# Root, scaling and one weight piece moved, context subtractions split between two engines, exponentials kept in PSUM

## The reference

```python
kh = concat([ctx @ wk + bk, bias_k])            # per head, K = 128
vh = concat([ctx @ wv + bv, bias_v])
weights = softmax((h @ wq + bq) @ kh^T / sqrt(K))
x = x + (weights @ vh) @ wo + bo                # h = layernorm(x), layers 1 and 2
x = x + gelu(layernorm(x) @ w_fc1 + b_fc1) @ w_fc2 + b_fc2
```

## Time and profile before

| what | value |
|---|---|
| median of three runs | 1814.93 us (1812.28 to 1815.42) |
| profiled execution | 1819.03 us |
| its span | 1817.2 us |
| VectorE busy | 1180.4 us |
| ScalarE busy | 743.2 us |
| GpSimd busy | 823.0 us |
| PE weight loads (beside matmuls) | 1724.6 us |

### The profile page before, as it was taken

One profiled execution on the slowest core, in us unless ns is written; L12 is line 12 of the kernel. 1 busy time (PEld: TensorE's weight loads), 2 busy tenths in 40 slices (PEclk: granted clock), 3 DMA queues, 4 the chain that ended last, 5 costly groups with the idle time before them and its releaser, 6 DMA issues.

```text
span 1817.2 us, 30212 instructions
## 1 busy us (share of the span) xinstructions
PE 1773.7 (98%) x11146; PEld 1724.6 (95%) x11146; DVE 1180.4 (65%) x2711; ACT 743.2 (41%) x1624; POOL 823.0 (45%) x653
## 2 busy tenths in 40 slices
PE   8999999999999999999999999999999999999999
PEld 4899999999899999998989999998999999999999
DVE  2667666666776665666775666667766656576665
ACT  3644333334443333335443343335433333344554
POOL 2684352353283352532672523532833525325554
PEclk9999999999999999999999999999999999999999
DMA  9833231123441221223521211234412212204342
GB/s 249 241 118 90 66 86 45 49 65 107 112 125 39 55 59 46 77 63 100 144 72 44 74 44 54 60 107 116 120 38 55 60 45 78 63 18 141 117 128 82
DMA packets 116164, 156.89 MB, mean 86 GB/s; under 512 B 48344, under 2 KB 63960, under 8 KB 116020
## 3 DMA queue, kind: packets, MB, share of 16 engines
q1 hardware_dynamic: 113300, 150.68, 29.7%
q10 hardware_dynamic: 2720, 4.30, 0.7%
HBM read 149.81 MB, written 5.14 MB: 85 GB/s over the span
## 4 chain that ended last, share of the span: by engine, by line
PE 79%; DVE 7%; DMA 5%; POOL 4%; ACT 3%; issue 1%; SPq 1%; ACTq 0%; DVEq 0%; POOLq 0%
PE psum L680 25%; PE psum L681 25%; PE psum L682 25%; PE psum L1004 3%; POOL wbuf_lo L597 2%; DMA stage<-head_w_dram 1%; DMA ctxT_in<-ctxT_dram 1%; DMA p_scratch<-p_row 1%; DVE prob L1811 1%; POOL wbuf_hi L553 1%; DVE a_lo L1510 1%; DMA ctx_rows_in<-ctx_dram 1%; ACT prob L1358 1%; POOL kw L581 1%; DVE stats L1802 1%
## 5 line engine op out<-in xcount | busy, mean ns | idle before, releaser
L553 POOL TENSOR_TENSOR wbuf_hi<-stage,zero_col 128x512 fp32r<-128x512 f32 x256 | 270.3, 1056 | 727.5 <-PE psum L682 613.5
L597 POOL TENSOR_TENSOR wbuf_lo<-stage,wbuf_hi 128x512 fp32r<-128x512 f32 x256 | 344.3, 1345 | 20.1
L680 PE MATMUL psum<-pT_hi,ctx_rows_hi 121*128 121x250 f32 (+3 forms) x1152 | 333.9, 290 | 0.0
L681 PE MATMUL psum<-pT_lo,ctx_rows_hi 121*128 121x250 f32 (+3 forms) x1152 | 331.4, 288 | 0.0
L682 PE MATMUL psum<-pT_hi,ctx_rows_lo 121*128 121x250 f32 (+3 forms) x1152 | 331.3, 288 | 0.0
L680 PE MATMUL psum<-ctxT_hi,a_hi 128*125 128x362 f32 (+1 forms) x832 | 281.2, 338 | 0.4
L682 PE MATMUL psum<-ctxT_hi,a_lo 128*125 128x362 f32 (+1 forms) x832 | 274.2, 330 | 0.0
L681 PE MATMUL psum<-ctxT_lo,a_hi 128*125 128x362 f32 (+1 forms) x832 | 274.1, 329 | 0.0
L680 PE MATMUL psum<-a_hi,wbuf_hi 128*128 128x400 f32 x720 | 258.0, 358 | 6.1 <-POOL wbuf_lo L597 4.5
L1510 DVE TENSOR_TENSOR a_lo<-psum,a_hi 128x500 fp32r<-128x500 f32 (+2 forms) x288 | 144.1, 521 | 174.8 <-ACT a_hi L1132 174.7
L681 PE MATMUL psum<-a_lo,wbuf_hi 128*128 128x400 f32 x720 | 250.0, 347 | 0.0
(11 more groups left out here) (196 smaller groups left out, 3465.0 us busy)
## 6 DMA issues: line engine op xcount, KB each, us to landing
stage<-head_w_dram SPq DMA_DIRECT2D x256, 256.0 KB, 2.7
mlp_stage<-mlp_w_dram SPq DMA_DIRECT2D x32, 512.0 KB, 3.5
ctx_rows_in<-ctx_dram SPq DMA_DIRECT2D x20, 726.0 KB
ctxT_in<-ctxT_dram SPq DMA_DIRECT2D x20, 724.0 KB, 6.9
p_b<-p_scratch SPq DMA_DIRECT2D x64, 200.0 KB, 3.6
key_stage<-head_w_dram SPq DMA_DIRECT2D x22, 256.0 KB, 8.8
l0w<-l_w_dram ACTq DMA_DIRECT2D x16, 256.0 KB, 8.6
x_held<-x_scratch SPq DMA_DIRECT2D x4, 800.0 KB, 5.7
```

The costliest lines, as they stand in the source:

```text
L553: return nc.gpsimd.tensor_tensor(out, in_, zero_col[0:in_.shape[0], :].broadcast_to(tuple(in_.shape)), ALU.add)
L597: nc.gpsimd.tensor_tensor(lo, held, hi.bitcast(F32), ALU.subtract).then_inc(stage_free, 1)
L680: pe.matmul(out, a_h, x_hi, start=start, stop=False)
L681: pe.matmul(out, a_h, x_lo, start=False, stop=False)
```

## The change

The pieces: q4 comes in step (0, 0) instead of (0, 1). GpSimd's context rows of batches 1 to 3 each come one weight later. The context subtractions are cut into parts: the rows into 3 of 512, the columns into 4 of 362. In three of the four phases GpSimd takes over the columns of batches 0 and 1 of the phase that follows, near the end of the phase; VectorE keeps those of batch 2 (behind k0) and 3 (now in step (0, 2)). The semaphore of the columns' low parts becomes one for each batch.

The exponentials are written back into the bank of the scores, and VectorE scales from there into `prob`. The wait for the transposes of two blocks ago goes from the exp to the scaling, and the scores' wait for their bank goes from the exp to the scaling.

In the step (5, 2) ScalarE does hidden_roots ahead of the second exp; in (5, 3) ctx_rows_hi of batch 0 goes to the end of the step and ctx_columns_hi of batch 1 comes there from behind the last attended_hi. On VectorE, at both steps, a part of attended_lo comes ahead of each invert or scale, and the fourth of these behind probs_lo.

```diff
-    (0, 0, "a"): "q3", (0, 1, "a"): "k3", (0, 1, "b"): "q4", (0, 2, "a"): "k4",
+    (0, 0, "a"): "q3", (0, 0, "b"): "q4", (0, 1, "a"): "k3", (0, 2, "a"): "k4",
...
-ROWS_LO_BEHIND = {9: 1, 10: 2, 11: 3}
+ROWS_LO_BEHIND = {10: 1, 11: 2, 12: 3}
...
             def ctx_rows_lo(use, b):
-                at = slice(3 * b, 3 * b + 3)
                 pool.wait_ge(cr_hi_s, use * NB + b + 1)
-                nc.gpsimd.tensor_tensor(r_lo[0:CH, at, :], r_in[0:CH, at, :], r_hi[0:CH, at, :].bitcast(F32),
-                                        ALU.subtract).then_inc(cr_lo_s, 1)
+                for at in range(3 * b, 3 * b + 3):
+                    done = nc.gpsimd.tensor_tensor(r_lo[0:CH, at, :], r_in[0:CH, at, :], r_hi[0:CH, at, :].bitcast(F32),
+                                                   ALU.subtract)
+                done.then_inc(cr_lo_s, 1)
+
+            def ctx_columns_lo(use, b):
+                pool.wait_ge(ct_hi_s, use * NB + b + 1)
+                ctx_b = slice(b * T, (b + 1) * T)
+                for c in range(DC):
+                    done = nc.gpsimd.tensor_tensor(c_lo[:, c, ctx_b], c_in[:, c, ctx_b], c_hi[:, c, ctx_b].bitcast(F32),
+                                                   ALU.subtract)
+                done.then_inc(ct_lo_s[b], 1)
...
                         if ph + 1 < len(PHASES):
+                            ctx_columns_lo(ph + TURNS, 0)
                             ctx_rows_lo(ph + TURNS, 0)
+                    if i == W_AT["v", H - 2] and ph + 1 < len(PHASES):
+                        ctx_columns_lo(ph + TURNS, 1)
...
-                    wait(pe, s_exp, ph * S_LAYER + i - 1)
+                    wait(pe, s_norm, ph * S_LAYER + i - 1)
...
                     act.wait_ge(s_max, ph * S_LAYER + i + 1)
-                    if i >= 2:
-                        act.wait_ge(pt_mm, ph * S_LAYER + T_AT[SCORED[i - 2]] + 1)
-                    else:
-                        wait(act, pt_mm, ph * S_LAYER)
                     st = stats[0:rows, i % 2, :]
-                    nc.scalar.activation(prob[0:rows, i % 2, :], bank[S_BANK + i % 2][0:rows, 0:T], ACT.Exp,
-                                         bias=st[:, 0:1], accum_out=st[:, 2:3]).then_inc(s_exp, 1)
+                    scored = bank[S_BANK + i % 2][0:rows, 0:T]
+                    nc.scalar.activation(scored, scored, ACT.Exp, bias=st[:, 0:1], accum_out=st[:, 2:3]).then_inc(s_exp, 1)
...
-                        exps(k, b, 1)
                         if (k, b) == VARIANCE_IN:
                             hidden_roots(ph)
-                        if (k, b) == STEPS[-1] and reload:
-                            ctx_rows_hi(ph + TURNS, 0)
+                        exps(k, b, 1)
...
                             ctx_columns_hi(ph + TURNS, 0)
+                        if (k, b) == STEPS[-1] and reload:
+                            ctx_rows_hi(ph + TURNS, 0)
+                            ctx_columns_hi(ph + TURNS, 1)
...
                 attended_hi(*before)
-                if reload:
-                    ctx_columns_hi(ph + TURNS, 1)
...
-                low(c_lo[:, :, ctx_b], c_in[:, :, ctx_b], c_hi[:, :, ctx_b]).then_inc(ct_lo_s, 1)
+                for c in range(DC):
+                    done = low(c_lo[:, c, ctx_b], c_in[:, c, ctx_b], c_hi[:, c, ctx_b])
+                done.then_inc(ct_lo_s[b], 1)
...
-                    nc.vector.tensor_scalar(prob[0:rows, i % 2, :], prob[0:rows, i % 2, :], st[:, 3:4], None, ALU.mult)\
+                    if i >= 2:
+                        dve.wait_ge(pt_mm, ph * S_LAYER + T_AT[SCORED[i - 2]] + 1)
+                    else:
+                        wait(dve, pt_mm, ph * S_LAYER)
+                    nc.vector.tensor_scalar(prob[0:rows, i % 2, :], bank[S_BANK + i % 2][0:rows, 0:T], st[:, 3:4], None, ALU.mult)\
                         .then_inc(s_norm, 1)
...
-                if ph > 0:
-                    ctx_columns_lo(ph + TURNS - 1, 0)
                 for kind, h in pieces("start"):
                     (queries_lo if kind == "q" else through_keys_lo)(h)
-                    if ph > 0 and (kind, h) == ("q", 1):
-                        ctx_columns_lo(ph + TURNS - 1, 1)
                     if ph > 0 and (kind, h) == ("k", 0):
                         ctx_columns_lo(ph + TURNS - 1, 2)
...
-                        if (k, b) == (0, 1) and ph > 0:
+                        if (k, b) == (0, 2) and ph > 0:
                             ctx_columns_lo(ph + TURNS - 1, NB - 1)
                         if (k, b) == VARIANCE_IN:
-                            for part in range(DC):
+                            for part in range(DC - 1):
+                                attended_lo(*before, part, part + 1)
                                 hidden_invert(ph, part, part + 1)
+                            attended_lo(*before, DC - 1, DC)
+                        elif (k, b) == SCALED_IN:
+                            for part in range(DC - 1):
                                 attended_lo(*before, part, part + 1)
-                        elif (k, b) == SCALED_IN:
-                            for part in range(DC):
                                 hidden_scale(ph, part, part + 1)
-                                attended_lo(*before, part, part + 1)
+                            attended_lo(*before, DC - 1, DC)
                         elif before is not None:
                             attended_lo(*before)
                         probs_lo(k, b, 0)
+                        if (k, b) == VARIANCE_IN:
+                            hidden_invert(ph, DC - 1, DC)
+                        if (k, b) == SCALED_IN:
+                            hidden_scale(ph, DC - 1, DC)
```

7 lines of the change are left out of this document (4 added, 3 removed).

## The result

The changed kernel takes 1821.26 us in the median of 12 runs, the kernel before 1815.18 us in 12 runs beside them: a ratio of 1.0042, 95% interval 1.0030 to 1.0053. It is slower by 0.4%, where 0.3% faster was forecast, and the time lies above the range. The profiled execution took 1826.60 us, the slowest of the twelve.

The account below looks back on a forecast made before the run. TensorE, busy 98% of the span, was taken as the bound, so only its waits counted. Gains of 20.1 us less losses of 13.9 gave -6.2, from 1814.9 to 1808.7 us; range 1794 to 1819.

Parts of the forecast that it names:

- Root: Hidden norm's root: tables and root ahead of the exp let VectorE start attended_lo 0.7 us earlier; gain 3.3 us.
- Scaling: Hidden norm's scaling: VectorE no longer held by GpSimd's context rows, the row copy ready in time; gain 6.6 us.
- First steps: First steps of phases 1 to 3: fewer context subtractions and q4's matmuls remove 6.05 us of waits; phase 0's 1.27 too.
- Scaled probabilities and xT: Scaling from PSUM no longer contends with GpSimd: gain 2.3 us on scaled probabilities, 0.6 on a transposed x at 228.
- k2 at the phase start: GpSimd gets in between VectorE's four column parts; PE waits 3.4 us in three phases, 10.2 against 4.5 before: +5.7.
- Single head: VectorE's four column parts let GpSimd in, so the low probabilities come late: loss 5.5 us.
- Turn: Turn of the phase: GpSimd's added columns mostly covered by its idle 5.48 us; 0.9 us at each of three, +2.7.
- opening figure of 40.8 us without a matmul: Whole span: the time in which PE does no matmul, the only time a step could change; 40.8 us.
- R2: Rival, chance 0.17: GpSimd's weight queue becomes the bound at the turn, 5 us each instead of 0.9; slower, 1821 us.
- Its sign: Turn: PE's total wait for wbuf_lo above 12 us would show the rival of GpSimd's weight queue.
- R1: Rival, chance 0.17: VectorE keeps the ports between its four parts, single head and phase start cost nothing; 1794.8 us.
- R3: Rival, chance 0.08: scaling from PSUM still waits for GpSimd, or holds its bank so scores wait; 1814 us.

Follow-up runs that it names:

- e8: Changed kernel with VectorE's columns of a batch in one instruction and ScalarE's high part of the context rows back in mid-step (5, 3): 1798.7 us, ratio 0.9908.
- e7: Changed kernel with VectorE's columns of a batch in one instruction and batch 1 of the columns given back to VectorE: 1802.5 us, ratio 0.9929.
- e5: Changed kernel with VectorE's columns of a batch in one instruction and p_b's load ahead of the last context rows: 1813.4 us, ratio 0.9990.
- e9: Changed kernel with VectorE's columns in one instruction and the 726 KB context rows' load behind the last but one weight and p_b: 1810.2 us, ratio 0.9974.

## Why the prediction was wrong

Two things failed: the wait at the turn of the phase, which was mis-sized, and TensorE's clock, for which the sum had no term. By its own steps, waits in the profiled executions:

- Root: 3.3 us forecast, 7.33 to 3.77 measured, 3.6. Right.
- Scaling: 6.6 forecast. The three waits of 2 us are gone, but 0.44 us for the last turn's low part and 0.44 for attended_lo came at each of three turns: 4.0. I had looked only at the copy that was late, and put ScalarE's two context parts before the last turn at nothing; its high part came late enough.
- First steps: 6.05 forecast and got in phases 1 to 3. Phase 0's 1.27 wasn't: 0.98 and 0.48 us stand there, since q4 covers one of two row copies.
- Scaled probabilities and xT: 2.9 forecast, 0.2 got. The scaling no longer waits for GpSimd, but at 595 ns instead of 0.41 it comes 0.19 us late where PE wants it at once, eight times 0.2 to 0.4. The price of 0.11 was too low: its lower bound of 413 ns follows from no row, and the 0.62 us that 400 columns from PSUM took the earlier trace rows lay nearer. "A turn away from PE nearly everywhere" was false at the eight places that matter.
- k2 at the phase start: the mechanism (GpSimd let in between the parts, on record as four context subtractions with GpSimd's between them) was right, the size forecast at 10.2, measured 8.0. (528.4 less 525.06 is 3.3, not 3.4, so the sum itself should have said 10.0.)
- Single head: likewise right, 5.5 forecast and 3.0 measured. The wait of 2.15 us near 43, which I had let grow, went instead.
- Turn: 0.9 us each forecast, 2.86, 2.58 and 2.87 measured, 5.6 us too little in all. This is the step that failed among the waits. I counted 3.9 us of columns against 5.48 us of idle time and left out that I had myself taken the rows' 3.8 us to the same place as a gain of the scaling; together they are 8.5 (3.79 + 4.73). The idle time that I had counted on now lay in front of them. What then costs is that each late split requests its next weight into the large load; e8 and e7, in which GpSimd is earlier, lose these waits.

These sum up to +1.1 us of waiting instead of -6.2 (the spans say +1.4). The other 6.2 us of the profiled executions were in no step at all: the clock. (In the timed runs the clock is worth about 3 us by its means. With 1.4 us of waits that makes 4.4 of the 6 to 8 us between the two kernels; the remainder is not accounted for.) The stretches at 1.2 GHz stood in the trace of before behind its waits of 2 us, and I read them only as waits. With the pauses that I had forecast (six of 2.6 to 3.4 us where seven of before were followed by a stretch) the term would have been small. In the profiled execution it is the three pauses at the turn, missed as waits, that bring four of the eleven stretches: 5.6 us of waits too little and 6.8 of clock are 12.4 of the 13.8 us between forecast and measured span.

The opening figure of 40.8 us without a matmul is wrong as well, since the earlier trace rows gives 1817.2 - 1773.7 = 43.5; nothing hung on it.

R2 named the turn, with "slower" and 1821 us. It had the place and the total: 2.8 us of wait and 2.3 of clock (four stretches of 1.7 over three turns) are 5.0 us a turn, which was its price, but half of it by another mechanism. Its sign, over 12 us of waits for wbuf_lo, did not appear: the changed kernel's list has no such wait. That 1821 was hit is partly luck, for the other terms were off by up to 2.7 us either way and nearly cancelled. R1 (VectorE keeps the ports) is refuted. R3's first half, that the scaling from PSUM might still wait, is refuted as well.

Left open: why some pauses are followed by one stretch, some by two, and two in eight by none, and why the clock fell near 110 us with no pause ahead.

## What to carry to other kernels

Price a pause of TensorE by its length: eight pauses of 1.1 us cost about what they last and left the clock alone, while eight of 2.0 or 2.9 us also lowered it, by 0.4 and 0.7%. So a change that gathers many small waits into a few long ones can lose although the waits sum up the same. Where two-input subtractions of VectorE and GpSimd hold each other up, cut GpSimd's long instructions and keep VectorE's whole: a part is an offer to the other engine. When work is moved off one place, add it to everything else that the same change moves to the new place, and look at the requests (here the next weight's load) that hang on it.

## What the runs showed of the hardware

- A scaling of 125 x 362 by VectorE takes 407 ns at the least and 3210 at the most from SBUF, and 593 to 599 from PSUM in all 208 cases. ScalarE's exp takes 563 ns from PSUM to SBUF and 537 back to PSUM.
- After a pause of TensorE of 2.0 us or more, the granted clock mostly stands at 1.2 GHz for 3.4 us, at times 6.8, though TensorE is then busy. In the 19 traces, without e5's and without the wait for the first load, this followed 55 of 64 pauses of 2.0 us or more, 10 of 18 of 1.6 to 2.0, and none of 78 of 1.0 to 1.6. In eight traces it also happened near 110 us with no such pause ahead. The loss is 1.7 us for each 3.4. It accounts for most of the spread between the changed kernel's runs: of the 10.6 us between its fastest and slowest (clocks 0.996 and 0.990) the clock's share is 10.9, with clocks that are rounded to 0.001, or 1.8 us.
- A weight of 256 KB requested while 726 KB are under way took about 8.1 us to land (issued at 497.74, and GpSimd started on it at 505.81 in e9), where the median is 2.8.
